# A gated expert stage with its gate and up weights copied to a ring in SBUF and standing in TensorE

## What is computed

```python
probs = softmax(xf @ Wr)                      # 4096 tokens, 16 experts
topk_p, topk_i = top_k(probs, 2)
y_e = silu(xf @ Wg[e]) * (xf @ Wu[e]) @ Wd[e] # D = 256, F = 128
routed = sum over the two chosen experts of topk_p * y_e
shared = silu(xf @ Sg) * (xf @ Su) @ Sd
x = x + routed + shared
```

## Time and profile before

| what | us |
|---|---|
| median of three runs | 1645.22 |
| the profiled execution | 1644.97 |
| its span in the profile | 1643.2 |
| first turn of x in the second expert stage | at 1444.89 |
| last scatter of that stage | at 1584.44 |
| first matmul of `finish` | at 1587.28 |

### The profile page before, as it was taken

How to read it: one execution, slowest core, us unless ns; L and a number is a source line. 1 busy time by engine, 2 the same in 40 slices (tenths; PEclk the granted TensorE clock), 3 DMA queues, 4 the chain that set the end, 5 groups by cost and what they waited for, 6 DMA issues and landing times. The chain is left out here.

```text
span 1643.2 us, 31228 instructions
## 1 busy us (share of the span) xinstructions
PE 1487.4 (91%) x9905; PEld 1114.3 (68%) x9905; DVE 1018.6 (62%) x3468; ACT 736.6 (45%) x1544; POOL 572.3 (35%) x994
## 2 busy tenths in 40 slices
PE   5999999983999999699799999999999597589987
PEld 3776676772999999565566666666666386468876
DVE  3345555453444444499898888888886286645558
ACT  3444444430222222345177777777777242244420
POOL 4123333344222222245532332322333165635530
PEclk9999999986999999899899999999999798889999
DMA  7001111115777777668857666667761575745556
GB/s 234 1 26 36 49 46 52 39 58 157 212 212 213 212 212 212 211 229 259 203 75 98 98 90 90 92 89 98 98 89 40 143 240 187 171 129 156 161 159 220
DMA packets 150592, 221.74 MB, mean 135 GB/s; under 512 B 23648, under 2 KB 98144, under 8 KB 150304
## 3 DMA queue, kind: packets, MB, share of 16 engines
q1 hardware_dynamic: 127904, 170.58, 45.2%
q0 software_dynamic: 13344, 36.55, 6.4%
q10 hardware_dynamic: 9184, 12.61, 2.5%
HBM read 141.16 MB, written 78.25 MB: 134 GB/s over the span
## 5 line engine op out<-in xcount | busy, mean ns | idle before, releaser
L2095 ACT ACTIVATE t_probs<-t_ps_st 128x512 f32<-128x512 f32 x576 | 313.2, 597 | 124.9 <-PE t_ps_st L2147 122.4
L2073 DVE CUSTOM_DVE_ANT_0 whole_sum<-t_ps_s,t_later 128x512 bf16<-128x512 f32 (+3 forms) x512 | 285.5, 586 | 14.0 <-PE t_ps_s L2133 11.9
L2049 POOL TENSOR_SCALAR_AFFINE_SELECT t_probs<-t_probs 128x128 f32<-128x128 f32 x512 | 137.4, 300 | 330.5 <-ACT t_probs L2095 328.9
L2133 PE MATMUL t_ps_s<-t_ks,t_qs 96*128 96x512 f32 (+3 forms) x768 | 247.8, 362 | 0.5 <-ACT t_neg_max L2085 0.5
L2147 PE MATMUL t_ps_st<-t_qs,t_ks 128*128 128x512 f32 (+3 forms) x768 | 242.7, 365 | 0.8 <-ACT t_probs L2095 0.8
L2147 PEld LDWEIGHTS t_ps_st<-t_qs,t_ks 128*128 128x128 f32 x768 | 136.8, 189 | 73.6 <-ACT t_probs L2095 40.2
L2073 DVE CUSTOM_DVE_ANT_0 whole_sum<-t_ps_s,t_later,t_first_max 128x512 bf16<-128x512 f32 (+3 forms) x256 | 140.5, 549 | 47.8 <-PE t_ps_s L2133 47.8
L2162 PE MATMUL t_ps_o<-t_probs,t_vs 128*17 128x256 f32 (+1 forms) x2560 | 154.9, 361 | 0.5 <-ACT whole_sum L2102 0.5
L2133 PEld LDWEIGHTS t_ps_s<-t_ks,t_qs 96*128 96x128 f32 x768 | 138.7, 190 | 18.0 <-DVE t_first_max L2073 1.6
L1460 POOL DMA_INDIRECT outputs_dram<-m_y,m_place x71 | 68.1, 959 | 208.8 <-DVE m_place L1535 201.1
L1490 PE MATMUL m_ps_h<-m_xt,m_w_t 128*128 128x128 f32 x1136 | 140.7, 278 | 0.0
(11 more groups left out here) (340 smaller groups left out, 2652.1 us busy)
## 6 DMA issues: line engine op xcount, KB each, us to landing
m_w_t<-in_w_dram SPq DMA_DIRECT2D x71, 512.0 KB, 4.4
t_qs<-qkt_dram SPq DMA_DIRECT2D x128, 128.0 KB, 5.6
t_ks<-qkt_dram SPq DMA_DIRECT2D x128, 128.0 KB, 5.7
m_x_t<-gathered_dram SPq DMA_DIRECT2D x79, 128.5 KB, 2.1
m_x_t<-gathered_dram SPq DMA_DIRECT2D x71, 129.0 KB, 2.1
d_ye<-outputs_dram SPq DMA_DIRECT2D x8, 1024.0 KB, 8.2
qkt_dram<-d_hi ACTq DMA_DIRECT2D x32, 256.0 KB, 5.2
qkt_dram<-d_lo SPq DMA_DIRECT2D x32, 256.0 KB, 7.2
```

Of the source, the lines that this page charges most:

```text
L2049: nc.gpsimd.affine_select(out=diag, in_=diag, compare_op=ALU.is_ge, fill=0.0, base=0, pattern=[[1, P]], channel_multiplier=-1).then_inc(ma ...
L2073: nc.vector.tensor_tensor_reduce(out=seen[:, (NP * p + x) % (RS + 1), 0:keys], in0=bank_of(p, x)[:, 0:keys], in1=masks, scale=1.0, scalar= ...
L2095: nc.scalar.activation(probs[:, p % 2, i // NST, base:base + STC], ps_st[(NX * p + i) % RT][:], ACT.Exp, scale=HD ** -0.5).then_inc(exp_re ...
L2133: nc.tensor.matmul(bank_of(p, x)[:, 0:keys], q[0:MAX_ROW, head, qc * P:(qc + 1) * P], k[0:MAX_ROW, head, k0:k0 + keys], start=True, stop=T ...
```

## The change

The phase's function is replaced by one for this mixture alone, `run_gated_experts`. ACT copies the gate and up weights of each tile's expert from `w_up` (the same tensor as `wgu_sb`) to a ring of three in SBUF, two steps ahead (`take_weights`), so ACT and no longer PE or DVE takes the address of the gate and up weights from a register. PE has these weights standing and turned x moving; the gated product comes out turned, and `turn_h` and `copy_h` are gone. The down product stays three steps behind. `ps_x` has two buffers; `sig`, `act_g`, `ht` and `ps_h` have three. SP's and POOL's programs stay as they are, as does DVE's `weights_of_choice`.

```diff
-    ps_x = pb(name + "ps_x", [P, KD, P])
-    ps_h = [pb(f"{name}ps_h{s}", [P, width]) for s in range(2)]
-    ps_ht = [pb(f"{name}ps_ht{s}", [P, blocks, P]) for s in range(2)]
+    w_t = sb("m1_w_t", [P, 3, KD, 2 * F1])
+    sig = sb("m1_sig", [P, 3, P])
+    act_g = sb("m1_act_g", [P, 3, P])
+    ht = sb("m1_ht", [P, 3, P])
+    ps_x = [pb(f"m1_ps_x{s}", [P, 2 * DM]) for s in range(2)]
+    ps_h = [pb(f"m1_ps_h{s}", [P, 4, P]) for s in range(3)]
...
             def go_up(t):
-                pe.wait_ge(xt_ready, t + 1)
-                wait(pe, h_ready, t - 1)
-                for j in range(KD):
-                    last = nc.tensor.matmul(ps_h[t % 2][:], xt[:, t % 2, j, :], w_up[:, j, bass.ts(expert[t], width)],
-                                            start=(j == 0), stop=(j == KD - 1))
+                pe.wait_ge(w_ready, t + 1)
+                pe.wait_ge(xt_ready, t + 1)
+                wait(pe, h_ready, t - 2)
+                for f in range(2):
+                    for j in range(KD):
+                        last = nc.tensor.matmul(ps_h[t % 3][:, f, :], w_t[:, t % 3, j, f * F1:(f + 1) * F1], xt[:, t % 2, j, :],
+                                                start=(j == 0), stop=(j == KD - 1))
                 last.then_inc(h_done, 1)
...
             for i in range(n_list + 3):
                 if live(i):
                     turn_x(i)
                 if live(i - 1):
                     go_up(i - 1)
-                if live(i - 2):
-                    turn_h(i - 2)
                 if i % 4 == 3 and live(i + 1):
                     look_up(i + 1)
                 if live(i - 3):
                     go_down(i - 3)
...
+            def gate(t):
+                dve.wait_ge(sig_ready, t + 1)
+                nc.vector.tensor_tensor(act_g[:, t % 3, :], ps_h[t % 3][:, 0, :], sig[:, t % 3, :], ALU.mult).then_inc(gated, 1)
+                dve.wait_ge(gated, t + 1)
+                wait(dve, y_done, t - 2)
+                nc.vector.tensor_tensor(ht[:, t % 3, :], ps_h[t % 3][:, 1, :], act_g[:, t % 3, :], ALU.mult).then_inc(h_ready, 1)
...
+            def take_weights(t):
+                if t % 4 == 0:
+                    expert.update(enumerate(entries(act, t, 0, E - 1), t))
+                wait(act, h_done, t - 2)
+                nc.scalar.activation(w_t[:, t % 3], w_up[:, :, bass.ts(expert[t], 2 * F1)], ACT.Copy).then_inc(w_ready, 1)
...
+            act.wait_ge(*weights)
+            take_weights(0)
+            take_weights(1)
+            for i in range(n_list + 1):
+                if live(i):
+                    copy_x(i)
+                if live(i - 1):
+                    sigmoid(i - 1)
+                if live(i + 2):
+                    take_weights(i + 2)
```

More of the change, by code:

```diff
@@ L2859, in build @@
               lambda eng: load_moe1_up(eng, moe1_loaded, wgu_sb, w_gu))
-        phase(run_experts, c, "m1_", E1, gathered[1], outputs[1], kept, (2 * F1, wgu_sb, None), (F1 // P, wd_sb, None),
-              (moe1_loaded, 16 * (KD + 1)), lambda dve, i: weights_of_choice(dve, nc, kept, i), by_row=True)
+        phase(run_gated_experts, c, E1, gathered[1], outputs[1], kept, wgu_sb, wd_sb,
+              (moe1_loaded, 16 * (KD + 1)), lambda dve, i: weights_of_choice(dve, nc, kept, i))
         phase(finish, c, outputs[1], kept, total, xnt_all, shared, flat(out))
```

264 lines of the change are left out of this document (104 added, 160 removed).

## The result

The changed kernel took 1633.65 us (median of five runs, 1629.39 to 1638.22), the kernel before 1645.27 us beside it (five runs, 1645.03 to 1647.08). In a later batch of runs the same change was slower; that comes in the experiments. Two executions of later batches took far longer than all others, 1940.41 and 2166.87 us; they count in the medians given for their kernels and in no ratio.

What follows compares the result with a forecast made beforehand. PE's own instruction stream was taken to bound the second expert stage. Shorter steps (-6.8), look-ups (-3.8) and start (-0.4) summed to -11.0 us, from 1645.22 to 1634.2 us, with a range of 1632.8 to 1639 us.

Steps and rivals of the forecast that it cites:

- What bounds the stage, the step and the look-up: Second expert stage: PE's own stream sets the pace; step falls to 1.54 us and look-ups cost nothing more.
- 6.8 + 3.8: Second expert stage: 6.8 us from 76 steps each 0.09 shorter, 3.8 us from 19 look-ups no longer costing 0.20.
- the rival of uncovered weight loads: Up product: eight load and matmul pairs take 2.4 us instead of 0.89, giving 1752 us; chance 0.01.
- ACT: ACT in the stage: 1.29 us a step by durations, weight copy 0.631, slack 0.7 us; busy about 6.7 of 8 us.
- look-ups still show: Rival: look-ups or ACT's register loads still cost 0.20 us each, 3.8 us come back, 1638.0 us; chance 0.18.
- ACT the bound: Rival: ACT's mean step passes 1.684 us, up to 1.90, making the kernel slower at 1662 us; chance 0.03.
- Tail: Stage's end: last scatter stays at the same distance from the last up product, so nothing gained.
- Start: Stage's start: two buffers let the second turn of x run beside the first copy, gaining 0.4 us.
- The rest of the kernel: Everything outside the second expert stage: claimed unchanged, adding nothing to the sum.
- some noise: Low end of the range, 1632.8 us: allowance beside 0.3 us of delays and a start giving twice as much.
- a side to which I gave 0.04: Forecast sign for the whole kernel: slower than before, chance 0.04, from the rivals ACT as bound and uncovered weight loads.

Runs made afterwards that it cites:

- The early look-up in the old form: Kernel before with PE's look-up of four experts moved ahead of the turn of h; 1640.5, 1643.3 and 1652.6 us against 1645.2, 1647.9 and 1657.2.
- with an operation more: Changed kernel with one more unused ACT copy of 128x256 from SBUF to SBUF in each step; stage 132.10 us, step 1.553 us.
- the first trace: First profile of the changed kernel, nothing further edited; its measured time was 1633.65 us against 1645.27 for the kernel before.
- its repeat: The changed kernel run and profiled again with nothing edited; 1631.77 us, stage 131.64 us.
- plain stores: Changed kernel with POOL's scatters replaced by plain transfers from SP, rows not brought to their tokens; ratio 0.9905 where the kernel before took 1657.19 us.
- the first batch: Follow-up runs on chip 1: changed kernel repeated, early look-up, no weight copy, one more ACT copy; kernel before about 1645 us.
- at 1.99: Changed kernel with two more unused ACT copies of 128x512 in each step; even steps of 1.99 us, in a batch with the kernel before at 1658 us.
- fifth: Batch on chip 1 repeating plain stores, plain stores with six loads, and the old stage with early look-up; kernel before 1657.19 us.
- fourth batch: Batch on chip 3 with plain stores, plain stores with six loads, and the old stage with early look-up; kernel before 1647.92 us.
- third batch: Batch on chip 10 with both kernels unedited, dummy PE turns, and down product two steps behind; unedited changed kernel 1669.23 us, ratio 1.0063.

## Why the prediction was right and wrong

**What bounds the stage, the step and the look-up: right.** 1.544 us a step against 1.54, and 117.32 us for 76 steps, 10.65 less than before, against 6.8 + 3.8 = 10.6. The early look-up in the old form alone gave the 3.8 back as 4.1. Eight pairs of load and matmul took 0.89 as the first expert stage had promised; the rival of uncovered weight loads (1752) is gone.

**ACT: right in cost, wrong in size.** Its copies cost nothing (131.15 without, 131.64 with). The copy has 0.626 us as taken, but I added durations where starts count, and took 0.49 to 0.70 for a register load of 0.31. ACT is busy 5.73 of 8 us, not 6.7. The load is hidden in idle time (0.28), and costs 0.10 where there is none. The rivals "look-ups still show" and "ACT the bound" were further off than their chances said; with an operation more the stage still kept 1.553.

**Tail: right.** Last up product to `finish` was 8.54 and is 8.47.

**Start: mis-sized.** Forecast 0.4; measured 1.24 in the first trace (5.88 against 4.64 us from first turn to third up product) and 0.25 in its repeat. Over all traces that way took 4.5 to 5.6 us in the changed stage and its forms with plain stores, and 5.4 to 6.2 in the old one. The granted clock rises somewhere in it, at a time that varies (0.97 from 1444 to 1448 us in the first trace of the changed kernel, 0.69 from 1448 to 1452 before), which hides the second buffer's share: with a single `ps_x` the way took 5.92 us, in another batch than the 5.62 of the kernel with two.

**The step that failed: the low side of the range, with the start and the rest of the kernel as the terms under it.** The mechanism held, and two terms were sized too small for what was measured. The start stood in the sum with 0.4 us and twice that in the range, and the first trace had 1.24. The rest of the kernel stood in it with nothing ("the rest unchanged"), and the first trace won 3.4 us in `front`, in code that did not change. Against both the range had only "some noise", about 0.7 us. It rested on three runs of the kernel before that lay within 2.1 us; in the first batch 21 runs of that same kernel spread from 1639.17 to 1652.52. So the stage came out 12.0 us shorter in the first trace and 10.7 in the repeat, where 11.0 were forecast, and the time of 1632.77 fell just under a range 1.4 us deep on that side. Its own interval of 1630.1 to 1635.4 holds the forecast: how close or far the number came is as much luck as merit.

**What I did not see at all: the stalls.** In the one batch with the kernel before at 1657 to 1658 where it ran unedited, the same edit loses 0.6%, a side to which I gave 0.04, and for another mechanism (ACT as the bound). The trace of before had the row that probably mattered, POOL's scatters with 1.26 us each; I checked only that they fit into 1.54 us, not what they might do to their neighbours, and no trace of the first batch shows anything of it. The old stage, slower by 0.09 us a step and richer in waits, stalls seldom (1.701 a step); the new one, at 1.55, nearly every third step (1.836); at 1.99 not at all.

**Open.** Why the indirect scatters, if it is they, disturb in some batches and not in others; whether the matmul's end, its signal or ACT's start is late; and why 1.55 us a step suffers so much more than 1.63. It could be how closely one scatter follows the other, or the pace of signals beside them. A new stage slowed to 1.63, or with a scatter for every two tiles, would tell these apart; neither was tried. It does not go by the number of the chip: number 1 had 1645 in the first batch and 1657 in the fifth. The run that would settle the scatters' part, the changed kernel unedited and with plain stores in one batch of 1657, is missing.

## What to carry to other kernels

Cost a pipelined block by the distance of starts, on ACT as on PE, and look where the register load stands in the stream before rebuilding the stage: moving one look-up gave a third of the gain here, and was faster in all three batches where it ran. A change that takes slack from a pipelined stage, above all one beside POOL's indirect scatters, is not finished when it is faster in one batch; run it in several, on several chips, with the kernel before beside it. And take the width of a range from many runs, not from three that agree.

## What the runs showed of the hardware

The same program takes 1645 to 1648 us in some batches and 1657 to 1658 in others, with nearly the same granted clock (0.953 in the mean of the kernel before's executions in the first and fourth batch, 0.949 to 0.950 in the other three). Of the 15.9 us between the spans of the kernel before's two profiles 8.5 sit in `back`, where the granted clock was lower too (0.80 against 0.87 from its first matmul to the stage), and 1.6 in this stage (142.39 against 143.99), while the first expert stage and attention do not differ by more than 1. `back` alone does not tell the two apart: it took 131.0 to 132.7 us, but also 135.6 and 137.1, in the batches of 1645 to 1648, and 136.9 to 143.4 in the others. In the third batch ACT's sigmoid waited for PE's product up to 2.7 us, in the first trace and with plain stores at most 0.5. ACT's operations overlap by about 0.1 us (0.52 from start to start with a duration of 0.63; where ACT never rests the duration reads 0.70 to 0.81 and the distance stays 0.52). By the Trainium skill, page "ScalarE: Activation LUTs", section "What ACT_TABLE_LOAD costs", back-to-back ACTIVATEs overlap by about 93 ns; the rows agree with 0.09 to 0.11.
